# Causal attention in units of four heads with scores in tiles of 32 rows, and constant products on TensorE at the edges of stages

## The reference

```python
scores = jnp.einsum('bhqd,bhkd->bhqk', q, k) / sqrt(HD)
scores = jnp.where(causal, scores, -inf)
attn = jax.nn.softmax(scores, axis=-1)
out = jnp.einsum('bhqk,bhkd->bhqd', attn, v)      # L2f: three heads of k and v, each for four of q
x = x + out.reshape(B, S, 192) @ w_out
```

## Time and profile before

| | us |
|---|---|
| median of three runs | 1346.76 |
| lowest and highest | 1346.36, 1351.72 |
| profiled execution | 1348.67 |
| span of the profile | 1346.4 |
| mean granted clock of TensorE | 0.878 |

### The profile page before, as it was taken

The page is one execution under the profiler, slowest core; times in us unless marked ns, Lnnn a source line. Parts: engine busy times, 40 slices in busy tenths (PEclk is TensorE's granted clock), DMA queues, the critical chain, the costliest instruction groups (busy, mean ns, idle before and its releaser), DMA issues. The chain is left out here.

```text
span 1346.4 us, 25252 instructions
## 1 busy us (share of the span) xinstructions
PE 1056.4 (78%) x9184; PEld 678.7 (50%) x9184; DVE 660.2 (49%) x1822; ACT 407.7 (30%) x904; POOL 124.4 (9%) x181
## 2 busy tenths in 40 slices
PE   0999999988988789798786089917978978359991
PEld 0677667656565566556474034413735644324440
DVE  5271335414344465657576266634743662535552
ACT  2123222321414444334242022202421431025550
POOL 2000000000000000000100423350000000040013
PEclk9998999988999898889787589967978989569995
DMA  9200000000000000060000511127000000021113
GB/s 250 72 3 3 1 1 3 2 1 2 2 2 2 1 1 1 21 297 2 0 1 1 194 51 55 47 59 290 1 1 0 1 1 0 32 93 55 55 54 91
DMA packets 28875, 58.89 MB, mean 44 GB/s; under 512 B 3238, under 2 KB 24967, under 8 KB 27755
## 3 DMA queue, kind: packets, MB, share of 16 engines
q1 hardware_dynamic: 25592, 49.20, 10.6%
q0 software_dynamic: 3072, 7.34, 1.6%
q10 hardware_dynamic: 114, 1.04, 0.3%
HBM read 42.66 MB, written 14.81 MB: 43 GB/s over the span
## 5 line engine op out<-in xcount | busy, mean ns | idle before, releaser
L219 PE MATMUL banks<-xT,weights 96*96 96x512 f32 (+3 forms) x288 | 144.1, 650 | 1.2 <-ACT xT L620 0.9
L1337 ACT ACTIVATE work<-banks,nmax 128x128 f32<-128x128 f32 (+1 forms) x288 | 105.5, 418 | 106.9 <-DVE nmax L1376 106.8
L2015 DVE COPY gw<-gu 128x1152 f32 x104 | 81.6, 826 | 74.8 <-issue 48.0
L1376 DVE TENSOR_REDUCE nmax<-banks 128x2 f32<-128x256 f32 (+1 forms) x144 | 80.1, 556 | 63.8 <-PE banks L1281 61.3
L1256 PE MATMUL banks<-K,Q 96*128 96x128 f32 (+1 forms) x384 | 84.7, 347 | 11.6 <-PEq L92 11.6
L219 PEld LDWEIGHTS banks<-xT,weights 96*96 96x96 f32 (+3 forms) x288 | 52.0, 188 | 72.6 <-issue 65.1
L1942 PE MATMUL banks<-gw,sxT 128*64 128x384 f32 x416 | 82.2, 518 | 1.1 <-DVE gw L2015 0.9
L692 ACT ACTIVATE work<-banks 98x1024 f32<-98x1024 f32 (+1 forms) x48 | 49.2, 1024 | 108.9 <-PE banks L559 108.9
L559 PE MATMUL banks<-Q,K 64*98 64x196 f32 (+2 forms) x960 | 73.3, 291 | 9.6 <-ACT work L692 9.5
L1385 DVE COPY work<-banks 128x256 f32<-128x256 f32 (+1 forms) x144 | 79.1, 549 | 0.5
L1965 PE MATMUL banks<-dw,ehT 128*64 128x192 f32 x624 | 65.2, 346 | 14.6 <-ACT y L2000 11.1
(11 more groups left out here) (260 smaller groups left out, 1759.6 us busy)
## 6 DMA issues: line engine op xcount, KB each, us to landing
xin<-slots_in SPq DMA_DIRECT2D x52, 128.0 KB, 2.0
gu<-in_L2f_gu SPq DMA_DIRECT2D x1, 5760.0 KB, 17.9
gu<-in_L3f_gu SPq DMA_DIRECT2D x1, 5184.0 KB, 15.6
slots_out<-y SPq DMA_DIRECT2D x52, 96.0 KB
dn<-in_L2f_dn SPq DMA_DIRECT2D x1, 4608.0 KB, 28.5
slots_in<-zeros SPq DMA_DIRECT2D x1, 3584.0 KB, 23.5
gu<-in_L2f_gu SPq DMA_DIRECT2D x1, 3456.0 KB, 11.5
dn<-in_L3f_dn SPq DMA_DIRECT2D x1, 2592.0 KB, 21.3
```

The lines of the kernel that those rows point to most:

```text
L219: ins = nc.tensor.matmul(out, lhs(k, rows), rhs(k, rows), start=(k == 0), stop=(k == 1))
L1337: ins = nc.scalar.activation(w.Pr[0:rows, s % 3, hh, 0:lay.width(t)], S(s)[0:rows, hh, 0:lay.width(t)], ACT.Exp, bias=w.nmax[0:rows, s % 4 ...
L1376: nc.vector.tensor_reduce(w.nmax[0:rows, s % 4, :], S(s)[0:rows, :, 0:lay.width(t)], AX.X, ALU.max, negate=True).then_inc(max_ready, 1)
L2015: ins = nc.vector.tensor_copy(w.gw[:, par, b, :], w.gu[:, bass.ds(e, 1), :].rearrange("p o f -> p (o f)"))
```

## The change

`attend` takes units of four heads (12 units in a stage, `GROUPS, IN_GROUP = 3, 4`). K and Q are read in slices of 32 rows, two heads in a slice; `own` keeps one of the two heads, so there are four scaled copies of Q instead of twelve. The four heads' scores lie in two banks, a slice's two heads in one bank. PSUM: two units of scores (four banks), one bank for each 128 keys of transposed probabilities, one of outputs. VectorE copies the first 128 keys, ScalarE those of the far 128 (`copied_far`). Probabilities have two buffers instead of three. Steps follow each other at shorter distance (`U + 9`), and VectorE's small steps come three or four at a time.

`keep_busy` issues products of the constant bf16 identity and mask, 128 x 256, into a bank that is not read. There are 312 of them: 8 at the end of each `attend`, 14 or 10 at the end of each `causal_project` (14 with rotary tables), 14 in `turn_second_image` (feed-forward of both pairs and routing of L2f) between the transposes of the first and of the second image, 44 in `causal_setup` before L3a behind the third quarter of the gather, 36 and 28 in `sort_tokens`, 12 at the start of `experts`. For the 36 the scatter is issued in two parts with a semaphore between. In L2f the keys, rotated queries and `rb` move into the buffer of the last four experts' weights, where Q stood with six.

```diff
+def keep_busy(nc, env, bank, n):
+    out = env.banks[:, bank, 0:2 * P].rearrange("p (b q) -> p b q", b=2)
+    for _ in range(n):
+        nc.tensor.matmul(out, env.ident16[:, :], env.mask16[:, :, :], start=True, stop=True)
 ...
+    keep_busy(nc, env, 7, 14)
     pe.wait_ge(normed, 1)
 ...
-            for s in range(U + 10):
+            for s in range(U + 9):
                 if s < U:
-                    m, t, hp = units[s]
-                    if s >= 3:
-                        pe.wait_ge(exp_ready, s - 2)
-                    for hh in range(2):
-                        h = 2 * hp + hh
-                        for r0, rn, win in lay.parts(t):
-                            ins = nc.tensor.matmul(S(s)[r0:r0 + rn, hh, 0:lay.width(t)], lay.q(m, t, h, win),
-                                                   lay.k(m, t, h, win), start=(hh == 0 or kind != "causal"),
+                    m, t, g = units[s]
+                    if s >= 2:
+                        pe.wait_ge(exp_ready, s - 1)
+                    q0, n = m * TOKENS + t * P, (t + 1) * P
+                    for r in range(2):
+                        for b in range(2):
+                            c, i = divmod(2 * g + b, 3)
+                            rows = slice(32 * i, 32 * i + 32)
+                            nc.tensor.matmul(S(s)[:, b, r, 0:n], w.Q[rows, 2 * c + r, q0:q0 + P],
+                                             w.K[rows, c, m * TOKENS:m * TOKENS + n], start=(r == 0), stop=False, skip_group_check=True)
+                    for b in range(2):
+                        ins = nc.tensor.matmul(S(s)[:, b, :, t * P:(t + 1) * P], env.ident16[:, :], env.mask16[:, :, :],
+                                               start=False, stop=True, skip_group_check=True)
+                    ins.then_inc(scores_ready, 1)
                 u = s - 2
                 if 0 <= u < U:
-                    if u >= 2:
-                        pe.wait_ge(copied, u - 1)
+                    if u >= 1:
+                        pe.wait_ge(copied, u)
+                    if t == 1 and wide[u]:
+                        pe.wait_ge(copied_far, wide[u])
 ...
+            pe.wait_ge(exp_ready, U)
+            keep_busy(nc, env, 0, 8)
 
         @block.scalar
 ...
+                u = s - 2
+                if 0 <= u < U and units[u][1] == 1:
+                    act.wait_ge(turned, u + 1)
+                    if u >= 2:
+                        act.wait_ge(pv_done, u - 1)
+                    nc.scalar.activation(w.PT[:, u % 2, 1, :, :], PTb(1), ACT.Copy).then_inc(copied_far, 1)
 ...
-                for _ in range(0 if s < 2 else 2 if s >= U or (both and s % 2) else 1):
+                for _ in range(0 if s < 2 else 4 if behind_eps is not None else 3):
                     if next(ahead, "done") == "done" and behind is not None:
                         next(behind, None)
 ...
@@ causal_project
+            if rope:
+                pe.wait_ge(bank_read, 4)
+            keep_busy(nc, env, 4 if rope else 7, 14 if rope else 10)
@@ causal_setup
+                pe.wait_ge(gathered[2], 64)
+                keep_busy(nc, env, 7, 44)
@@ sort_tokens
+            if w.shared:
+                keep_busy(nc, env, 7, 28)
+            else:
+                pe.wait_ge(mostly_issued, 1)
+                keep_busy(nc, env, 7, 36)
@@ experts
+            keep_busy(nc, env, 7, 12)
```

More of the change, by code:

```diff
@@ L1205, in attend @@
-def attend(nc, env, w, kind, ip, inner, into_x, behind_eps=None, behind_centre=False):
+GROUPS, IN_GROUP = 3, 4
+def attend(nc, env, w, ip, inner, into_x, behind_eps=None):
     R, banks, ident = env.R, env.banks, env.ident
-    lay = Layout(kind, w)
-    HP = HEADS // 2
-    units = [(m, t, hp) for m in range(PAIR) for t in range(lay.tiles) for hp in range(HP)]
+    units = [(m, t, g) for m in range(PAIR) for t in range(2) for g in range(GROUPS)]
     U = len(units)
-    ck = lay.chunk()
+    wide = [sum(t for _, t, _ in units[0:n]) for n in range(U + 1)]
@@ new lines, in _ @@
+                    for c in range(t + 1):
+                        for j in range(IN_GROUP):
+                            ins = nc.tensor.transpose(PTb(c)[:, j, :], w.Pr[:, u % 2, j, c * P:(c + 1) * P], ident[:, :])
+                    ins.then_inc(turned, 1)
+                u = s - 3
+                if 0 <= u < U:
+                    m, t, g = units[u]
+                    tile = u // GROUPS
+                    pe.wait_ge(copied, u + 1)
+                    if t == 1:
+                        pe.wait_ge(copied_far, wide[u + 1])
+                    if g == 0 and tile >= 1:
+                        pe.wait_ge(O_out, tile)
+                    for c in range(t + 1):
+                        for j in range(IN_GROUP):
+                            h = IN_GROUP * g + j
+                            ins = nc.tensor.matmul(O[32 * j:32 * j + VW, g, :], w.V[:, m * 2 + c, h * w.kv_heads // HEADS, :],
+                                                   w.PT[:, u % 2, c, j, :], start=(c == 0), stop=(c == t))
+                    ins.then_inc(pv_done, 1)
@@ L1296, in _ @@
+                tile = ends_tile(s - 4)
                 if tile is not None:
-                    m, t, _ = units[s - 6]
-                    rows = lay.rows(t)
+                    m = units[s - 4][0]
                     pe.wait_ge(O_out, tile + 1)
@@ L1367, in _ @@
             behind = None
-            both = kind == "causal" and behind_eps is not None
-            for s in range(U + 10):
+            for s in range(U + 9):
                 if s < U:
-                    _, t, _ = units[s]
-                    rows = lay.rows(t)
+                    n = (units[s][1] + 1) * P
                     dve.wait_ge(scores_ready, s + 1)
@@ L1410, in _ @@
                         dve.wait_ge(added, 1)
[L1411 removed]
+                        behind = normalise_steps(nc, chain, env.s, env.xn, R, behind_eps, False, tiles=(0, 2))
+                tile = ends_tile(s - 4)
+                if tile is not None:
+                    dve.wait_ge(om_turned, tile + 1)
+                    if tile >= 2:
+                        dve.wait_ge(o_turned, tile - 1)
+                    chain(nc.vector.reciprocal(w.rsum[:, tile % 2, :], OM[:, :, HD]))
+                    nc.vector.tensor_tensor(w.On[:, tile % 2, :].rearrange("p (h d) -> p h d", d=HD), OM[:, :, 0:HD],
+                                            w.rsum[:, tile % 2, :, None].to_broadcast([P, HEADS, HD]),
+                                            ALU.mult).then_inc(normed, 1)
+                for _ in range(0 if s < 2 else 4 if behind_eps is not None else 3):
+                    if next(ahead, "done") == "done" and behind is not None:
+                        next(behind, None)
             for _ in ahead:
@@ L1438, in causal_project @@
     per = 2 if rope else 1
-    act_heads = [(c, j) for c in range(2) for j in range(6) if (j >= 2 if rope else c == 0)]
-    dve_heads = [(c, j) for c in range(2) for j in range(6) if (c, j) not in act_heads]
     with stage(nc, env.names) as (block, sem):
@@ L2455, in _constants @@
     c["cos"], c["sin"] = (np.tile(a.T, (CH // HD, 1)).astype(np.float32) for a in (cos, sin))
-    c["own"] = np.kron(np.eye(CH // HD), np.full((HD, 1), QSCALE)).astype(np.float32)
+    c["own"] = np.tile(np.kron(np.eye(2), np.full((HD, 1), QSCALE)), (3, 1)).astype(np.float32)
     return c
```

249 lines of the change are left out of this document (75 added, 174 removed).

## The result

The changed kernel took 1369.65 us in the median of four runs (1362.54 to 1379.58) against 1347.4 us before. The ratio is 1.016, with a 95% interval of 1.008 to 1.025. 1322 us were forecast, and the time lies above the range. The profiled execution (span 1360.5 us) was the fastest of the four. Some executions of these kernels, at a lower granted clock, took over 1.5% longer than the fastest of the same kernel: the ratios leave them out, the medians do not.

The account below looks back on a forecast made before the run. TensorE was taken to bound the middle of the attention stages, a chain through all engines their end. Terms -11 + 5 - 7 - 12 = -25 us from 1348.7 profiled, median 1.9 lower: 1322 us; own range 1308 to 1334, overall 1290 to 1351.

Parts of the forecast that it names:

- The step that failed: Start of each attention stage: a 1.1 us hole before unit 2 was foreseen, with no clock loss priced there.
- the first 8 us of each stage at clock 1.0: Sign to look for in the trace: full granted clock at the start of every attention stage.
- Rival (b): Clock falls inside attention stages: 4.5 us each, 27 in all, 1358 us; decides above 4 us a stage; chance 0.17.
- the middle hole: TensorE pause of 1.7 us between units 6 and 7 of a stage, where transposes wait for ScalarE's far copy.
- TensorE's own work: Attention stages: a wide unit of four heads takes 2.8 us against 3.49, a narrow one 1.7 against 2.0.
- rival (a): Attention scores in 32-row tiles run one after the other: 27 us in all, 1348 us, no change; chance 0.10.
- The list of twelve units: Score start times of an attention stage's units, followed from 0 to 26.2 us.
- The loop of 3.24 us a unit: Wide attention units: scores, maximum, exponentials, far copy, transposes and values take 6.5 us for two units, keeping 0.25 of 0.7 saved.
- under 2.9 us: Sign against the forecast: wide attention units following each other faster than this would mean the loop is mispriced.
- The stages' sum: Six attention stages: -11 from new units, +5 from end products, -7 from stage starts at full clock.
- The eight end products: Constant products at each attention stage's end delay the next stage by 0.8 us, +5 us in all.
- The constant products: 312 products at stage ends and edges: +5 cost, -7 at attention starts, -12 at other edges by holding the clock.

Follow-up runs that it names:

- x5: Changed kernel plus twenty constant products of 128 rows behind the second unit's masks at each stage's start; 1328.44 us, ratio 0.987 to the kernel before.
- x8: x2 with each score product reading only the 32 rows of its pair of heads instead of 96; 1491.27 us, ratio 1.097 to the kernel before.
- x2: Kernel before, old attention kept, plus the 312 constant products alone; 1333.63 us, ratio 0.990.
- x14: x5 without the eight constant products at each attention stage's end and the wait ahead of them; 1330.18 us, ratio 0.986 to the kernel before.
- x6: x5 with ScalarE's far copy issued ahead of the exponentials of the same step; run again, 1317.63 us, ratio 0.975 to the kernel before.
- x4: Changed kernel with scores over all 96 rows and twelve copies of Q, units of four heads kept; 1350.2 us, ratio 1.000 to the kernel before.
- x9: Changed kernel with 96-row scores and ScalarE's far copy ahead of the exponentials; 1337.59 us, ratio 0.992 to the kernel before.
- x12: x10 with the twenty products of x5 at each stage's start; run again, 1321.01 us, ratio 0.978 to the kernel before.
- x10: x9 with 32-row score pairs in the wide units (256 columns), 96 rows in the narrow ones; 1326.42 us, ratio 0.984 to the kernel before.
- m1: Kernel before plus two product streams in the sorting's idle time, 96 rows then 32 rows; clock rose after 3.8 us in the first, stayed at 0.50 in the second.
- m2: m1 with the two streams in the other order, 32 rows then 96; the clock again rose only with 96 rows, after 4.4 us.
- m3: m1 with other streams: 64 rows on both halves in turn, then 128 rows with 17 result columns; clock rose after 3.6 and 4.5 us.

## Why the prediction was wrong, point by point

- **The step that failed** is the clock inside the new stage. The forecast had narrow 32-row units and a hole of 1.1 us before unit 2 at each stage's start and priced the clock there at nothing ("the first 8 us of each stage at clock 1.0"). Measured, it fell 1.6 to 3.7 us in, in all six. Rival (b) let the clock fall, at the middle hole, and priced that at "about 2.5 us" a stage from the earlier trace rows (10.8 over five stages is 2.2). Those rows hold 96-row products. With 32-row products the way back took 13.7 to 20.5 us instead of 3.4 to 6.8, and the stages cost 34.7 us more than x5's (308.8 against 274.1), 5.8 a stage. Rival (b) had the right sign, its threshold of 4 us a stage and a time (1358) 12 us short; the place, the stage's first units and not the middle hole, and the cause, the rows of the products, were missing.
- **TensorE's own work** was right: 2.8 us for a wide unit, 2.83 by its pieces at full clock; the eight scores 0.96 and a change of 0.10, 1.06 measured; two abreast, so rival (a) is out. The page of the Trainium skill "TensorEngine Tiling (Array Packing)", Tiling Modes, says that different tiles can run their loads and products in parallel, and the trace agrees (7 ns apart). What the 32 rows did to the clock is another matter: by the ratios x8 is 11% longer than x2.
- **The list of twelve units** was right where the clock held. x5's first stage starts its units at 0, 1.0, 3.1, 4.5, 6.6, 9.0, 12.0, 16.4, 19.2, 21.2, 23.9, 26.4 us; the forecast had 0, 0.8, 3.0, 4.3, 6.5, 9.1, 12.0, 16.7, 19.3, 21.3, 23.8, 26.2. The loop of 3.24 us a unit, whose terms add to 4.95 and not 4.97, was too dear for what stands in the stage: only three wide units follow each other, the transposes under the first two are of narrow units, and the starts are 2.1 to 3.1 us apart, so the sign "under 2.9 us" came true. The list, made by hand, had this right. From the last scores to the end of the last projection x5 took 14.6 us, where 14.9 were forecast. The pause between the seventh and the eighth unit is there, 1.33 us and ended by ScalarE's copy of 128x512; ScalarE's row and TensorE's, of x5:

```profile
473.53 0.61 ACT L1289 ACTIVATE work<-banks 128x512 f32<-128x512 f32 x1
...
474.29 1.06 PE L1226 MATMUL banks<-small,work 128*128 128x128 f32 x8 [1.33 <-ACT work L1289]
```

- **The stages' sum.** Forecast -11 + 5 - 7 = -13; x5, which is the changed kernel with the clock held or soon back, has -16.5 (290.6 to 274.1), the twenty products included.
- **The eight end products** were put at +5. The changed kernel's rows (the earlier trace rows before) show them beside VectorE's sum, ending 1.0 us ahead of the next stage's first product, and x14 without them has the same time within its interval (0.986 against 0.987). They cost 0 to 1 us.

```profile
505.23 2.51 PE L229 MATMUL banks<-weights,OT 96*128 96x192 f32 x8 [0.47 <-ACT OT L1295]
507.54 1.81 PE L195 MATMUL banks<-mask,ident 128*128 128x256 bf16 x8
507.78 0.55 DVE L1321 TENSOR_TENSOR X<-X,banks 128x384 f32<-128x384 f32 x1 [3.50 <-PE banks L229]
510.35 1.05 PE L219 MATMUL banks<-small,ahead 128*96 128x128 f32 x8 [1.01 <-PEq L92]
```

- **The constant products** were put at +5 - 7 - 12 = -14 and gave -13.7 alone (x2, interval -18 to -9). By place it was -4.7 in the stages (ends included) and -8.0 in the rest. In the changed kernel the stages took as long with the products as without (308.7 and 308.1), since the clock fell 1.6 to 3.7 us in all the same, and the rest is 4 us less than before. The start of the feed-forward shows how one edge works, answering to the earlier trace rows: at 0.50 for 11.3 us of 989.5 to 1000.8 before, for 3.9 us after.

```profile
1003.60:1007.50 3.90, 3.90 (x18) 2.62 (x18) 3.35 (x19) 1.41 (x2) 0.00 (x0) 0.51 0.00 0
1007.50:1014.40 6.90, 5.86 (x17) 2.78 (x17) 1.00 (x3) 1.86 (x3) 0.00 (x0) 1.00 0.00 0
```

- **What stays open.** The far copy first gained more than its place shows: 1.0 to 1.1 us a stage between the seventh and eighth unit (first stage: x5 4.4, x6 3.4), which is most of the 7.2 us in the stages' sum, and 17 us in the ratio (0.987 to 0.975). The part outside the stages (1052.1 to 1045.8 in the two profiles) I can't name. What makes the clock fall at a stage's start is shown only in part: with 96-row scores it mostly held (x4, x9), and x5's fill held it in three stages of six; but it fell before the pause as well as in it and behind it, so the pause is not the cause by itself. Four 32-row tiles at once were not tried.

x5, with twenty products of 128 rows more at each stage's start, took 1328.4 us, which lies in the forecast's range.

## What to carry to other kernels

TensorE busy without a pause is no proof that its clock will be granted: read the granted clock by the kind of product before narrowing products to tiles of 32 rows, and try the kind in an idle stretch first. Where 32-row tiles do save time, start them with TensorE at full clock, fill the holes ahead of and among the first of them with products of the full array, or keep the 96-row form for the units at the stage's start (x12 and x10 did; x10 still fell once in six stages). A price for "the clock falls" has two parts, how often it falls and what work has to bring it back, and the second comes from rows of the same kind of work or is unknown.

## What the runs showed of the hardware

- Streams of f32 products of 256 columns, begun at 1.2 GHz, TensorE busy throughout: with 96 rows the clock rose to 2.4 GHz after 3.8 and 4.4 us (m1, m2), with 64 rows on both halves after 3.6, with 128 rows and 17 result columns after 4.5 (m3). With 32 rows, two tiles at once, it did not rise in 10.6 us (m1, m2).
- In whole stages with 32-row scores among other work the clock stood at 1.2 GHz for 68 us in three stages, unbroken work in the one shown, and for 27.3 us in the other three (x8, one score after the other), and for 13.7 to 20.5 us (changed kernel, two abreast). Once at full, the clock stayed there through wide units with 32-row pairs (x5, x10). The page of the Trainium skill "TensorE: Matmul & The Clock Gate", The HAM clock gate, says that the clock follows how busy TensorE has been; the 96-row streams agree, and x8 and the 32-row streams do not: there TensorE was busy in 68.30 of 68.30 us and in 10.58 of 10.60, and the clock stayed down. The measurement decides.
- Two 32-row tiles started 7 ns apart, and eight such instructions of 256 columns with the change of form behind them took 1.06 us, as the 0.97 us and a change of the 64-row tiles of the earlier trace rows would.
